# Layer 1's point-cloud loop: VectorE makes the low part of 4 of 16 slots, from a high part that ScalarE copies to PSUM; GpSimd makes the rest

## The chip, the cores and the metric

One core of a Trainium2 chip runs the whole program in one launch. The metric is device time in microseconds (us), the median of the runs. Names in the profile: PE is TensorE's matmuls and PEld its weight loads, DVE is VectorE, ACT is ScalarE, POOL is GpSimd, SP is the engine that issues most DMAs. L1894 is line 1894 of the kernel file.

## What is computed

Two rows of 64 tokens (1024 wide) go through six residual blocks: a quantised cross product, a state-space mixer, a mixture of LoRA experts, a point-cloud attention, a block-sparse product and a gated feed-forward block. The change lies in the fourth, the point cloud. Its 1024 points (per batch entry, with 64 features each) are sorted by four space-filling keys, and every point looks at a window of 10 neighbours in each order:

```python
neigh = gather(feats, inds)
gf = jnp.concatenate([jnp.broadcast_to(center, (B, N, k, C)), neigh - center], axis=-1)
...
qh = x16.reshape(B * N, k, nheads, headdim)
scores = jnp.einsum('bihd,bjhd->bhij', qh, qh) / np.float32(np.sqrt(headdim))
attn = jax.nn.softmax(scores, axis=-1)
out = jnp.einsum('bhij,bjhd->bihd', attn, qh).reshape(B * N, k, total)
fused = out @ W_lin.T + b_lin
...
h1 = _lrelu(_instance_norm(h1, (2, 3)))
feats1 = h1.max(axis=-1)
```

This is done twice (layer 1 and layer 2), the second time on the features that the first gave; then one more convolution joins both.

## The kernel before

**Where the loop stands.** Each layer first sorts (one-hot products on TensorE) and then runs a loop of 43 steps, 24 points a step. The five engines each run their own program; semaphores alone order them. `walk` writes out the first 8 and the last 3 steps (and 6 more to drain) and turns the 32 between into a hardware loop of four steps a turn, so each engine takes a branch once in four steps. `lagged(n)` means that an engine works n steps behind the loop's number.

**What one step does, by engine** (all tiles have 128 partitions; a step's weights are 16 slots of 30 columns, 480 in all):

- GpSimd, step *it*: `normalise(it)` multiplies the exponentials S by the reciprocal row sums (L2043); `differences(it + 3)` makes the 960 neighbour-minus-centre values X of three steps ahead (L2025); `low_part(it)` subtracts the rounded weights from S and rounds the rest (L2050).
- ScalarE, step *it*: `high_part(it - 1)` rounds S to 16 bits (L1782), `exponentials(it)` (L1789), `unload(it - 4)` copies the weighted rows out of PSUM (L1774), and then a transposing DMA of X is issued (L1796).
- VectorE, step *it*: `reduce(it - 6)` takes statistics and a maximum of the finished rows (L1874, L1880); `shift(it)` takes the maximum of the scores and subtracts it (L1892, L1894); `turn(it - 2)` transposes the weights in 32 x 32 blocks (L1907); `denominators(it)` sums the exponentials and takes the reciprocal (L1914, L1916).
- TensorE, step *it*: `scores(it)` (L1586, L1594), `weighted_rows(it - 4)` (L1614), `linear(it - 5)` (L1635, L1643).
- SP, step *it*: four DMAs place the transposed weights P_turned into PT, a block-diagonal tile (L1523).

**High and low part.** The 32-bit weights are used as two 16-bit halves, interleaved in PP: index 0 of the last axis is the rounded value, index 1 what the rounding left. The products of both are added on TensorE. The two lines in question:

```python
sc.copy(c.PP[ph % 2][:, :, 0:ROWS, 0], c.S[ph % 2][:, :, :]).then_inc(s_hi, 1)
...
gp.tensor_tensor(PP[:, :, 0:ROWS, 1], c.S[ph % 2][:, :, :], PP[:, :, 0:ROWS, 0], ALU.subtract).then_inc(s_lo, 1)
```

**Who waits for whom.** S, PP, P_turned and PT exist twice, so `shift(it)` waits for the low part of step it - 2 (semaphore c_P_low), `turn(it)` for the low part of its own step, `normalise(it)` for the reciprocal (c_den), `low_part(it)` for the high part (c_P_high), `weighted_rows(it)` for the DMAs into PT and for the unload of the step before. The scores have one set of PSUM banks (0, 1), the weighted rows banks 3 and 4, the finished rows 5 and 6. Banks 2 and 7 are used while sorting and not in the loop's even part.

Of the kernel before, what the change touches and what calls it, by code (L numbers as in the profile page):

```python
# [9 lines left out]
ALU = mybir.AluOpType  # L10
# [1249 lines left out]
FIRST = 2 * PHASES  # L1260
LAST = 3
EARLY = STEPS - 5
SOON = N // 4
AHEAD = 3
TURN_LAG, PV_LAG, LINEAR_LAG, REDUCE_LAG = 2, 4, 5, 6
# [89 lines left out]
class Cloud:  # L1355


    def __init__(self, k, ctx):
        sb = lambda name, shape, dt=F32: k.sb(name, shape, dt, ctx)
        made = k.cloud  # L1360
        self.iota, self.PP, self.rows_u, self.cols_v = made.iota, made.PP, made.rows_u, made.cols_v
        self.X_more = [k.hT[:, 4 * u:4 * u + 4, :].bitcast(F16) for u in range(PHASES - len(made.X))]
        self.X, self.X_zeros = made.X + self.X_more, k.sem("c_X_zeros")
        self.conv_d, self.blocks, self.f16, self.WC = made.conv_d, made.blocks, made.f16, made.WC
        slots = lambda first, count: k.ring[:, first:first + count, :].rearrange("p a n -> p (a n)")
        self.spl = slots(9, 1).bitcast(F16).rearrange("p (s t c) -> p s t c", s=2, t=NT)
        self.both = sb("f16_both", [P, B, N + STEP], F16)
        self.fsg = slots(7, 2).rearrange("p (t d) -> p t d", t=NT)
        self.fsg_late = slots(10, 1).rearrange("p (t d) -> p t d", t=NT // 2)
        self.W = N + WIN - 1 - LEAD  # L1370
        self.fsT = sb("sortedT", [P, 4, self.W])
        self.pre = sb("first_windows", [P, 4, LEAD, WIN])
        self.fTr = k.ring[:, 0:4, :]
        self.S = [sb(f"S{u}", [P, 2 * SLOTS, ROWS]) for u in range(2)]
        self.mx = [sb(f"mx{u}", [P, 2 * SLOTS]) for u in range(2)]
        self.den = [sb(f"den{u}", [P, 2 * SLOTS]) for u in range(2)]
        self.PT = k.PT
        self.PC = [sb(f"P_turned{u}", [P, 2 * SLOTS, 32, 2], F16) for u in range(2)]
        self.XR = [x.rearrange("p (s d) -> p s d", s=SLOTS) for x in (slots(7 + u // 2, 1).bitcast(F16)[:, u % 2 * N:(u % 2 + 1) * N] for u in range(PHASES))]
        self.OT = [sb(f"OT{u}", [P, 2, B, COLS]) for u in range(2)]  # L1380
        self.step_sems = [k.sem(f"c_{i}") for i in ("X", "scores", "max", "shifted", "exp", "den", "P", "P_high", "P_low", "P_turned",
                                                    "PV", "O", "H", "reduced")]
        self.placed = [k.sem(f"c_P_placed{u}") for u in range(2)]
        self.rows_in = [k.sem(f"c_X_rows{u}") for u in range(PHASES)]
        self.order_sems = [k.sem(f"c_{i}") for i in ("split", "f16", "second_parts", "centre_copied", "perm",
                                                     "ordered", "rows", "sorted_turned", "sorted_copied", "windows")]
        self.layer_sems = [k.sem(f"c_{i}") for i in ("std", "early_statistics", "first_centres")]
        self.weight_sems = k.sem("c_weights"), k.sem("c_weights_rest")
        self.rows_kept, self.kept = k.rows_kept, k.sem("c_rows_kept")
        self.stats = sb("stats", [P, B, STEPS, 6])  # L1390
        self.partial = sb('early_mean_variance', [P, B, 2])
        self.mvb, self.stdb, self.rsb, self.shift, self.cb = sb("mvb", [P, B, 2]), sb("stdb", [P, B]), sb("rsb", [P, B]), sb("shift", [P, B]), sb("cb", [P, 1])
        self.bias, self.o_bias = sb("end_bias", [P, B]), sb("o_bias", [P, 1])
        self.end_sems = [k.sem(f"c_end_{i}") for i in ("bias", "scaled")]
        self.f1, self.f2 = k.ring[:, 4, :], k.ring[:, 5:7, :]
        self.lin_n, self.lin_c, self.conv, self.blin = made.lin_n, made.lin_c, made.conv, made.blin

        self.o_stats, self.o_mv, self.o_std, self.o_rs = sb("o_stats", [P, 2, 6]), sb("o_mv", [P, 2]), sb("o_std", [P, 1]), sb("o_rs", [P, 1])
        self.conv_2, self.flag = sb("conv3_last", [P, C]), sb("block_flags", [P, KC * 32])
        self.conv3_in = k.sem("conv3_in")  # L1400
        self.WN = sb("WN", [P, 2, B, P])

        self.wparts, self.wrest = sb("WC_parts", [P, 3, P], BF16), sb("WC_rest", [P, P])


def stage_cloud_layer(nc, k, dr, c, layer):
    O = C * layer
    nb = 1 if layer == 1 else B
    with ExitStack() as ctx:
# [31 lines left out]
        t0 = STEPS * (layer - 1)  # L1441
        s_PT, s_XR = c.placed, c.rows_in

        def placed(it, ph):

            before = (layer - 1) * (STEPS - STEPS // 2 if ph % 2 == 0 else STEPS // 2)
# [12 lines left out]
        if layer == 2:  # L1459
            s_both = sem("f16_both")  # L1460
            s_early = sem("early_products")
            s_conv, s_ost, s_ostd, s_ox = (sem(i) for i in ("last_convolution", "out_statistics", "out_std", "out_x"))
            res = c.fsg[:, 0:NT // 2, :].rearrange("p t d -> p (t d)")
        n = Norm(k, 3) if layer == 1 else None
        turns = n.turns if n else lambda count: count
# [215 lines left out]
        def _(act):  # L1681
# [94 lines left out]
            def high_part(it, ph):  # L1776
# [4 lines left out]
                    act.wait_ge(s_turned, t0 + it - 1)  # L1781
                sc.copy(c.PP[ph % 2][:, :, 0:ROWS, 0], c.S[ph % 2][:, :, :]).then_inc(s_hi, 1)  # L1782

            def exponentials(it, ph):
                if not inside(it):
                    return
# [11 lines left out]
            def step(it, lagged):  # L1798
                high_part(*lagged(1))
                exponentials(*lagged(0))  # L1800
                unload(*lagged(PV_LAG))
                turn_rows(*lagged(0))
                if isinstance(it, int) and it < NM - 1:
# [14 lines left out]
                    sc.activation(raw_piece(i), raw_piece(i), ACT.Identity, bias=c.bias[:, b:b + 1], scale=c.rsb[:, b:b + 1]).then_inc(s_scaled, 1)  # L1818
            if layer == 2:
                act.wait_ge(s_ost, 3)  # L1820
                sc.activation(c.o_std[:, :], c.o_mv[:, :][:, 1:2], ACT.Sqrt, bias=k.eps[:, 0:1]).then_inc(s_ostd, 1)
                act.wait_ge(s_bias, bias0 + 2)
                sc.activation(res[:, HALF:], ps[:, 1, :], ACT.Identity, bias=c.o_bias[:, 0:1], scale=c.o_rs[:, 0:1]).then_inc(s_scaled, 1)

# [2 lines left out]
        def _(v):  # L1827
# [68 lines left out]

            words = lambda x: x[:, :, :, :].rearrange("p s j w -> p (s j w)").bitcast(F32)

            def turn(it, ph):
                if not inside(it):  # L1900
                    return
                v.wait_ge(s_lo, t0 + it + 1)
                if draining(it):
                    v.wait_ge(s_PT[ph % 2], placed(it - 2, ph))
                elif after(it, 2):
# [12 lines left out]
            def step(it, lagged):  # L1918
                reduce(*lagged(REDUCE_LAG))
                shift(*lagged(0))  # L1920
                turn(*lagged(TURN_LAG))
                denominators(*lagged(0))
                if isinstance(it, int) and it > STEPS:
                    early_statistics(it)

# [39 lines left out]
            if layer == 2:  # L1965
# [2 lines left out]
                    vec.bn_stats(c.o_stats[:, half, :], ps[:, half, :]).then_inc(s_ost, 1)  # L1968
                v.wait_ge(s_ost, 2)
                vec.bn_aggr(c.o_mv[:, :], c.o_stats[:, :, :]).then_inc(s_ost, 1)  # L1970
                v.wait_ge(s_ostd, 1)
                vec.reciprocal(c.o_rs[:, :], c.o_std[:, :]).then_inc(s_ost, 1)
                v.wait_ge(s_ost, 4)
                vec.scalar_tensor_tensor(out=c.o_bias[:, :], in0=c.o_mv[:, 0:1], scalar=-1.0, in1=c.o_rs[:, :], op0=ALU.mult, op1=ALU.mult).then_inc(s_bias, 1)
# [15 lines left out]
        def _(pool):  # L1990
            gp = nc.gpsimd
            if layer == 1:
                for more in c.X_more:
                    gp.memset(more, 0.0).then_inc(c.X_zeros, 1)
                pool.wait_ge(k.PT_zeros, 32)
                pool.wait_ge(c.X_zeros, len(c.X_more))
            pool.wait_ge(s_soon, soon0 + 16 * B * NHEAD)

            def first_differences():
# [45 lines left out]
            def low_part(it, ph):  # L2045
# [1 line left out]
                    return  # L2047
                PP = c.PP[ph % 2]
                pool.wait_ge(s_hi, t0 + it + 1)
                gp.tensor_tensor(PP[:, :, 0:ROWS, 1], c.S[ph % 2][:, :, :], PP[:, :, 0:ROWS, 0], ALU.subtract).then_inc(s_lo, 1)  # L2050

            def step(it, lagged):
                normalise(*lagged(0))
# [116 lines left out]
```

## Time and profile before

| | us |
|---|---|
| median of 3 runs (994.27 to 994.8) | 994.58 |
| the profiled execution | 993.34 |
| its span in the profile | 991.7 |
| busy over the span: TensorE | 922.2 (93%) |
| VectorE | 733.9 (74%) |
| GpSimd | 452.0 (46%) |
| ScalarE | 392.1 (40%) |
| L2050, low part, 86 instructions (both layers) | 97.9, mean 1139 ns |
| L2043, normalise, 86 instructions | 86.7, mean 1008 ns |
| L1782, high part, 86 instructions | 66.9, mean 778 ns |

A busy share over the whole span mixes stages with different limits, so the table says little about one loop. Layer 1's loop lies between about 498 and 680 us of the span, layer 2's between about 714 and 905. The times of the profile are those of one execution; 993.34 - 991.7 = 1.64 us of it lie outside the profiled span.

### The profile page before, as it was taken

To read this page: it belongs to the slowest core of one execution; us is meant where nothing else is said; L and a number is where in the kernel's file an instruction comes from. 1 tells how busy PE (TensorE), PEld (TensorE's weight loads), DVE (VectorE), ACT (ScalarE), POOL (GpSimd) and SP (SyncE) were. 2 spreads that over 40 slices of the span, in tenths; PEclk is the share of its full clock that TensorE was granted. 3 is DMA by queue.
4 is the path that set the end of the run, shared out by engine and by line. 5 is a ranking of instruction groups with operands and counts; after the bars stand their busy time and mean duration, and the time that the engine had idled before them with its cause. 6 is when DMAs were issued, how large, how long until landed. Compare 5 with 4: busy or idle time off the path is not lost. (4 is left out here: it accounts for less than half of the span.)

```text
span 991.7 us, 36771 instructions
## 1 busy us (share of the span) xinstructions
PE 922.2 (93%) x15278; PEld 701.0 (71%) x15279; DVE 733.9 (74%) x1931; ACT 392.1 (40%) x679; POOL 452.0 (46%) x410
## 2 busy tenths in 40 slices
PE   4899899999999999999978988879989999999998
PEld 2799879696969687765965666657955656665695
DVE  7698738866657483897967989886879999997410
ACT  6343414141433323212354555554355555553010
POOL 1101212531211202020299999980499999986000
PEclk9999999999999999999998999999979999999999
DMA  9998797888878796566257666672357665662650
GB/s 365 407 408 308 259 337 261 294 304 295 312 273 308 258 353 224 188 260 255 93 89 128 130 141 134 134 138 63 109 104 126 127 127 125 126 128 46 262 247 22
DMA packets 148961, 204.95 MB, mean 207 GB/s; under 512 B 99409, under 2 KB 101137, under 8 KB 148498
## 3 DMA queue, kind: packets, MB, share of 16 engines
q1 hardware_dynamic: 55058, 172.06, 48.9%
q10 hardware_dynamic: 91392, 23.34, 14.2%
q0 software_dynamic: 2432, 8.42, 2.4%
q8 instruction: 59, 0.97, 0.4%
q14 instruction: 20, 0.16, 0.0%
HBM read 154.45 MB, written 1.61 MB: 157 GB/s over the span
## 5 line engine op out<-in xcount | busy, mean ns | idle before, releaser
L546 PEld LDWEIGHTS ps<-hT,ring 128*128 128x128 f32 x2304 | 258.1, 192 | 6.7 <-issue 5.7
L546 PE MATMUL ps<-hT,ring 128*128 128x128 f32 x2304 | 260.0, 275 | 0.8 <-ACT xc L692 0.8
L1614 PE MATMUL ps<-PT,ring 128*64 128x120 f16 x2752 | 100.0, 225 | 27.8 <-ACT OT L1774 14.1
L1782 ACT CAST PP<-S 128x480 f16<-128x480 f32 x86 | 66.9, 778 | 125.4 <-POOL S L2043 125.4
L1614 PEld LDWEIGHTS ps<-PT,ring 128*64 128x64 f16 x2752 | 87.0, 113 | 37.8 <-issue 27.4
L978 POOL TENSOR_TENSOR y_y<-y_z,sgate 128x512 f32<-128x512 f32 x16 | 20.1, 1272 | 193.0 <-DVE y_z L909 193.0
L579 PE MATMUL ps<-wt,y_n 128*128 128x512 f32 x224 | 99.4, 596 | 1.4 <-DVE xs L901 1.4
L2050 POOL TENSOR_TENSOR PP<-S,PP 128x480 f16<-128x480 f32 x86 | 97.9, 1139 | 5.7 <-ACT PP L1782 5.7
L2043 POOL TENSOR_TENSOR S<-S,den 128x480 f32<-128x480 f32 x86 | 86.7, 1008 | 16.9 <-DVE den L1916 15.8
L808 DVE SCALAR_TENSOR_TENSOR xc<-xpad,parg,xc 128x128 f32<-128x128 f32 x192 | 59.3, 372 | 42.2 <-ACT xc L692 41.0
L1774 ACT COPY OT<-ps 128x960 f32<-128x960 f32 x86 | 81.2, 944 | 12.5 <-PE ps L1614 12.5
L2025 POOL TENSOR_TENSOR X<-sortedT,ring 128x960 f16 (+1 forms) x42 | 79.4, 1891 | 0.5 <-DMA ring<-X 0.5
L1639 PE MATMUL ps<-OT,WN 128*128 128x480 f32 x172 | 77.9, 576 | 0.0
L2025 POOL TENSOR_TENSOR hT<-sortedT,ring 128x960 f16 (+2 forms) x42 | 77.4, 1842 | 0.0
L579 PEld LDWEIGHTS ps<-wt,y_n 128*128 128x128 f32 x224 | 41.4, 190 | 48.7 <-issue 48.6
L1892 DVE TENSOR_REDUCE mx<-ps 128x16 f32<-128x480 f32 x86 | 56.1, 652 | 17.5 <-PE ps L1594 8.8
L1789 ACT ACTIVATE S<-S 128x480 f32<-128x480 f32 x86 | 51.6, 600 | 32.8 <-DVE S L1894 32.6
L1914 DVE TENSOR_REDUCE den<-S 128x16 f32<-128x480 f32 x86 | 56.0, 651 | 11.2 <-ACT S L1789 8.3
L1874 DVE BATCH_NORM_STATS2 stats<-ps 128x240 f32 (+2 forms) x129 | 47.5, 396 | 21.8 <-PE ps L1639 9.5
L1907 DVE STREAM_TRANSPOSE P_turned<-PP 128x512 f32<-128x512 f32 x86 | 60.4, 702 | 3.0 <-PE ps L1614 2.4
L1894 DVE TENSOR_TENSOR S<-ps,mx 128x480 f32<-128x480 f32 x86 | 56.6, 658 | 3.0
L834 DVE TENSOR_SCALAR_CACHE_REDUCE junk<-krow,kcol 128x1024 bf16<-128x1024 f32 (+3 forms) x64 | 51.7, 808 | 0.6 <-DVE kcol L824 0.2
(328 smaller groups left out, 1478.6 us busy)
## 6 DMA issues: line engine op xcount, KB each, us to landing
ring<-in_w_in SPq DMA_DIRECT2D x36, 2048.0 KB, 9.3
wt<-in_w_out SPq DMA_DIRECT2D x14, 2048.0 KB, 7.8
PT<-P_turned SPq DMA_DIRECT2D x332, 64.0 KB
ring<-in_w SPq DMA_DIRECT2D x8, 1024.0 KB, 12.9
ctx_chunks<-in_ctx SPq DMA_DIRECT2D x4, 1024.0 KB, 8.8
krow<-keys_scratch POOLq DMA_DIRECT2D x8, 512.0 KB, 7.5
mchunk<-in_mask_t POOLq DMA_DIRECT2D x8, 512.0 KB, 8.7
ring<-in_w_out SPq DMA_DIRECT2D x2, 2048.0 KB, 8.0
```

The lines of the kernel that those rows point to most:

```text
L546: mm = nc.tensor.matmul(ps[:, bank, j * T:(j + 1) * T], weights[:, j, kc * P:(kc + 1) * P], k.hT[:, kc, :], start=kc == 0, stop=kc == KC - 1)
L579: mm = nc.tensor.matmul(ps[:, 6 + c, :], rows[:, j, :], weights[:, j, c * HALF:(c + 1) * HALF], start=j == 0, stop=j == GB - 1)
L808: vec.scalar_tensor_tensor(out=dst, in0=src, scalar=params(j, tap), in1=dst, op0=ALU.mult, op1=ALU.add).then_inc(s_cv, 1)
L1614: mm = nc.tensor.matmul(ps[half, out_bank(it) + slot // 4, at:at + 4 * ROWS], XR[:, slot, half], PT[:, :, r * SLOTS + slot, 0:ROWS, part], ...
L1639: mm = nc.tensor.matmul(H, c.WN[:, a, 0, :], OT[:, a, :, :], start=False, stop=a == 1)
L1774: sc.copy(c.OT[ph % 2][:, :, :, :].rearrange("p a b n -> p a (b n)"), ps[:, out_bank(it):out_bank(it) + 2, 0:2 * COLS]).then_inc(s_O, 1)
L1782: sc.copy(c.PP[ph % 2][:, :, 0:ROWS, 0], c.S[ph % 2][:, :, :]).then_inc(s_hi, 1)
L1894: vec.tensor_tensor(S[:, :, :].rearrange("p (r s) i -> p r s i", r=2), scores, fcopy(c.mx[u][:, :], [[SLOTS, 2], [1, SLOTS], [0, ROWS]]), ...
L1907: vec.transpose(words(c.PC[ph % 2]), words(c.PP[ph % 2])).then_inc(s_turned, 1)
L2025: ins = gp.tensor_tensor(fcopy(c.X[u][:, 0, 0:1], full(cnt)), fcopy(c.fsT[:, 0, bass.ds(it * STEP, 1)], trio(start, cnt, 1)), fcopy(c.fTr[ ...
L2043: gp.tensor_tensor(S, S, fcopy(c.den[ph % 2][:, :], [[1, 2 * SLOTS], [0, ROWS]]), ALU.mult).then_inc(s_P, 1)
L2050: gp.tensor_tensor(PP[:, :, 0:ROWS, 1], c.S[ph % 2][:, :, :], PP[:, :, 0:ROWS, 0], ALU.subtract).then_inc(s_lo, 1)
```

## The change

In layer 1 alone the 16 slots are divided. GpSimd makes the low part of slots 0 to 11 (360 columns). ScalarE, behind each step's exponential, copies the rounded high part of slots 12 to 15 (120 columns) from PP to PSUM, in bank 2 or 7 by the step's parity. VectorE, at the end of each step, subtracts that copy from S and writes the low part of these slots. The transpose waits for both. Two new semaphores, c_P_high_share and c_P_low_share, carry the order; two old ones are given up for them (X_zeros is counted on `filled`, and out_std on the layers' shared `std`), with the same waits.

```diff
+SHARE, SHARE_BANK = slice(12, 2 * SLOTS), (2, 7)
...
+        shared = layer == 1
+        shares = [k.ps[:, bank, 0:(SHARE.stop - SHARE.start) * ROWS].rearrange("p (s i) -> p s i", i=ROWS) for bank in SHARE_BANK]
...
+            def high_share(it, ph):
+
+                if not inside(it) or not shared:
+                    return
+                if after(it, 2):
+                    act.wait_ge(c.low_share, t0 + it - 1)
+                act.wait_ge(s_hi, t0 + it + 1)
+                sc.copy(shares[ph % 2], c.PP[ph % 2][:, SHARE, 0:ROWS, 0]).then_inc(c.high_share, 1)
...
                 high_part(*lagged(1))
                 exponentials(*lagged(0))
+                high_share(*lagged(1))
                 unload(*lagged(PV_LAG))
...
+            def low_share(it, ph):
+
+                if not inside(it) or not shared:
+                    return
+                v.wait_ge(c.high_share, t0 + it + 1)
+                vec.tensor_tensor(c.PP[ph % 2][:, SHARE, 0:ROWS, 1], c.S[ph % 2][:, SHARE, :], shares[ph % 2], ALU.subtract).then_inc(c.low_share, 1)
...
                 v.wait_ge(s_lo, t0 + it + 1)
+                if shared:
+                    v.wait_ge(c.low_share, t0 + it + 1)
...
                 denominators(*lagged(0))
+                low_share(*lagged(1))
...
-                gp.tensor_tensor(PP[:, :, 0:ROWS, 1], c.S[ph % 2][:, :, :], PP[:, :, 0:ROWS, 0], ALU.subtract).then_inc(s_lo, 1)
+                mine = slice(0, SHARE.start if shared else 2 * SLOTS)
+                gp.tensor_tensor(PP[:, mine, 0:ROWS, 1], c.S[ph % 2][:, mine, :], PP[:, mine, 0:ROWS, 0], ALU.subtract).then_inc(s_lo, 1)
```

VectorE's program in layer 1's hardware loop, one of the four steps of a turn, before (the line numbers are those of each kernel's own file; in brackets the semaphores waited for):

```order
L1874 ISA [waits c_H]
L1874 BN_STATS stats<-ps 128x6
L1880 ISA
L1880 TENSOR_REDUCE ring<-ps 128x24
L1888 REGISTER_ALU
L1892 TENSOR_REDUCE mx<-ps 128x16 [waits c_P_low,c_scores]
L1894 TENSOR_TENSOR S<-ps,mx 128x480 [waits c_max]
L1907 STREAM_TRANSPOSE P_turned<-PP 128x512 [waits c_PV,c_P_low]
L1914 TENSOR_REDUCE den<-S 128x16 [waits c_exp]
L1915 ISA
L1916 RECIPROCAL den<-den 128x16 [waits c_den]
```

The same step of VectorE's program in the changed kernel:

```order
L1889 ISA [waits c_H]
L1889 BN_STATS stats<-ps 128x6
L1895 ISA
L1895 TENSOR_REDUCE ring<-ps 128x24
L1903 REGISTER_ALU
L1907 TENSOR_REDUCE mx<-ps 128x16 [waits c_P_low,c_scores]
L1909 TENSOR_TENSOR S<-ps,mx 128x480 [waits c_max]
L1931 STREAM_TRANSPOSE P_turned<-PP 128x512 [waits c_PV,c_P_low_share,c_P_low]
L1938 TENSOR_REDUCE den<-S 128x16 [waits c_exp]
L1939 ISA
L1940 RECIPROCAL den<-den 128x16 [waits c_den]
L1919 TENSOR_TENSOR PP<-S,ps 128x4x30 [waits c_P_high_share]
```

One instruction of 4 x 30 columns now stands between the reciprocal and the next step's statistics, and the transpose has one semaphore more.

ScalarE's program for the same step, before (CAST at L1782 is the high part, COPY at L1774 the unload):

```order
L1782 CAST PP<-S 128x16x30 [waits c_P_turned,c_P]
L1787 REGISTER_ALU
L1789 ACTIVATE S<-S 128x480 [waits c_shifted]
L1774 COPY OT<-ps 128x960 [waits c_H,c_PV]
L1796 DMA_TRANSPOSE ring<-hT 128x8x128
```

And in the changed kernel:

```order
L1787 CAST PP<-S 128x16x30 [waits c_P_turned,c_P]
L1801 REGISTER_ALU
L1803 ACTIVATE S<-S 128x480 [waits c_shifted]
L1796 CAST ps<-PP 128x120 [waits c_P_high,c_P_low_share]
L1779 COPY OT<-ps 128x960 [waits c_H,c_PV]
L1810 DMA_TRANSPOSE ring<-hT 128x8x128
```

The copy to PSUM stands between the exponential and the unload, so the unload and the transposing DMA are issued behind it.

## Rows read from the trace of the kernel before

**Rows 1.** Stretch, its length; busy PE, PEld, DVE, ACT, POOL; clock; DMA share; GB/s.

```profile
556.00:656.00 100.00, 86.55 (x2834) 61.36 (x2830) 89.67 (x182) 53.97 (x78) 100.00 (x78) 1.00 0.65 136
```

**Rows 2.** GpSimd's timeline over layer 1's loop: start us, length us, what.

```profile
502.49 0.99 POOL L2043 TENSOR_TENSOR S<-S,den 128x480 f32<-128x480 f32 x1 [0.39 <-DVE den L1916]
...
521.84 0.99 POOL L2043 TENSOR_TENSOR S<-S,den 128x480 f32<-128x480 f32 x1
...
538.37 0.98 POOL L2043 TENSOR_TENSOR S<-S,den 128x480 f32<-128x480 f32 x1
...
551.84 1.00 POOL L2043 TENSOR_TENSOR S<-S,den 128x480 f32<-128x480 f32 x1
...
652.37 1.06 POOL L2043 TENSOR_TENSOR S<-S,den 128x480 f32<-128x480 f32 x1
653.32 1.94 POOL L2025 TENSOR_TENSOR X<-sortedT,ring 128x960 f16<-128x960 f32 x1
655.16 1.19 POOL L2050 TENSOR_TENSOR PP<-S,PP 128x480 f16<-128x480 f32 x1
656.22 1.07 POOL L2043 TENSOR_TENSOR S<-S,den 128x480 f32<-128x480 f32 x1
657.18 0.90 POOL L2025 TENSOR_TENSOR hT<-sortedT,ring 128x360 f16<-128x360 f32 x1
657.94 0.45 POOL L2030 MEMSET hT<- 128x344 f16 x1
```

**Rows 3.** Waits from 560 to 640: us in total, times, longest.

```profile
ACT PP L1782 <- POOL S L2043: 37.6, 21, 1.9
...
PE ps L1614 <- ACT OT L1774: 10.6, 20, 0.7
...
DVE mx L1892 <- POOL PP L2050: 1.2, 6, 0.2
```

**Rows 4.** VectorE's timeline, layer 1's loop, across a branch.

```profile
562.56 0.25 DVE L1916 RECIPROCAL den<-den 128x16 f32<-128x16 f32 x1
563.08 0.42 DVE L1874 BATCH_NORM_STATS2 stats<-ps 128x240 f32 x1 [0.26 <-issue]
...
563.72 0.65 DVE L1892 TENSOR_REDUCE mx<-ps 128x16 f32<-128x480 f32 x1
564.40 0.66 DVE L1894 TENSOR_TENSOR S<-ps,mx 128x480 f32<-128x480 f32 x1
...
565.83 0.65 DVE L1914 TENSOR_REDUCE den<-S 128x16 f32<-128x480 f32 x1 [0.15 <-ACT S L1789]
566.51 0.25 DVE L1916 RECIPROCAL den<-den 128x16 f32<-128x16 f32 x1
...
570.38 0.25 DVE L1916 RECIPROCAL den<-den 128x16 f32<-128x16 f32 x1
570.54 0.37 DVE L1874 BATCH_NORM_STATS2 stats<-ps 128x240 f32 x1
```

**Rows 5.** VectorE's timeline, layer 2's loop.

```profile
804.77 0.66 DVE L1894 TENSOR_TENSOR S<-ps,mx 128x480 f32<-128x480 f32 x1
...
806.10 0.65 DVE L1914 TENSOR_REDUCE den<-S 128x16 f32<-128x480 f32 x1
...
821.52 0.66 DVE L1894 TENSOR_TENSOR S<-ps,mx 128x480 f32<-128x480 f32 x1
```

**Rows 6.** VectorE's timeline, a small subtraction ahead of layer 2.

```profile
688.51 0.28 DVE L1839 TENSOR_TENSOR WC_rest<-ps,WC_parts 128x128 f32<-128x128 f32 x1
688.71 0.61 DVE L1293 TENSOR_SCALAR ring<-iota,rank 128x512 f16<-128x512 f16 x2
```

**Rows 7.** ScalarE's timeline, layer 1's loop.

```profile
607.67 0.60 ACT L1789 ACTIVATE S<-S 128x480 f32<-128x480 f32 x1
608.17 0.94 ACT L1774 COPY OT<-ps 128x960 f32<-128x960 f32 x1
```

**Rows 8.** TensorE's timeline, a stall early in layer 1's loop.

```profile
540.30 1.14 PE L1614 MATMUL ps<-PT,ring 128*64 128x120 f16 x32 [2.21 <-DMA PT<-P_turned]
```

More of the change, by code:

```diff
@@ L1362, in __init__ @@
         self.X_more = [k.hT[:, 4 * u:4 * u + 4, :].bitcast(F16) for u in range(PHASES - len(made.X))]
-        self.X, self.X_zeros = made.X + self.X_more, k.sem("c_X_zeros")
+        self.X = made.X + self.X_more
         self.conv_d, self.blocks, self.f16, self.WC = made.conv_d, made.blocks, made.f16, made.WC
@@ L1383, in __init__ @@
         self.placed = [k.sem(f"c_P_placed{u}") for u in range(2)]
+        self.high_share, self.low_share = k.sem("c_P_high_share"), k.sem("c_P_low_share")
         self.rows_in = [k.sem(f"c_X_rows{u}") for u in range(PHASES)]
@@ L1461, in stage_cloud_layer @@
             s_early = sem("early_products")
-            s_conv, s_ost, s_ostd, s_ox = (sem(i) for i in ("last_convolution", "out_statistics", "out_std", "out_x"))
+            s_conv, s_ost, s_ox = (sem(i) for i in ("last_convolution", "out_statistics", "out_x"))
             res = c.fsg[:, 0:NT // 2, :].rearrange("p t d -> p (t d)")
@@ L1820, in _ @@
                 act.wait_ge(s_ost, 3)
-                sc.activation(c.o_std[:, :], c.o_mv[:, :][:, 1:2], ACT.Sqrt, bias=k.eps[:, 0:1]).then_inc(s_ostd, 1)
+                sc.activation(c.o_std[:, :], c.o_mv[:, :][:, 1:2], ACT.Sqrt, bias=k.eps[:, 0:1]).then_inc(s_std, 1)
                 act.wait_ge(s_bias, bias0 + 2)
@@ L1970, in _ @@
                 vec.bn_aggr(c.o_mv[:, :], c.o_stats[:, :, :]).then_inc(s_ost, 1)
-                v.wait_ge(s_ostd, 1)
+                v.wait_ge(s_std, std0 + nb + 1)
                 vec.reciprocal(c.o_rs[:, :], c.o_std[:, :]).then_inc(s_ost, 1)
@@ L1993, in _ @@
                 for more in c.X_more:
-                    gp.memset(more, 0.0).then_inc(c.X_zeros, 1)
+                    gp.memset(more, 0.0).then_inc(k.cloud.filled, 1)
                 pool.wait_ge(k.PT_zeros, 32)
-                pool.wait_ge(c.X_zeros, len(c.X_more))
+                pool.wait_ge(k.cloud.filled, 16 + len(c.X_more))
             pool.wait_ge(s_soon, soon0 + 16 * B * NHEAD)
```

## The prediction

> **What bounds the kernel now.** The busy table by stretch comes first: in the 100 us from 556 to 656, the even part of layer 1's loop, GpSimd is busy 100.00, VectorE 89.67, TensorE 86.55, ScalarE 53.97, at a granted clock of 1.00 [rows 1]. So read GpSimd's timeline. Its three instructions of a step start one behind the other: normalise to differences 0.95 us, differences to low part 1.84, low part to the next normalise 1.06, together 3.85, and from the start at 551.84 to that at 656.22 there are 27 steps, 3.866 each [rows 2]. (Instructions overlap a little, so I count from start to start, not by length.) The waits say the same from the other side. ScalarE waited 37.6 us for GpSimd's normalise in 21 steps, VectorE's score maximum for GpSimd's low part in 6 of them, and TensorE 0.53 us a step for ScalarE's unload of the weighted rows [rows 3]. GpSimd itself waits for nobody there. A shorter low part therefore shortens the step until the next engine has no slack.
>
> That next engine is VectorE. What can its step shrink to? Follow its starts [rows 4]: row sums to reciprocal 0.68 (566.51 - 565.83), reciprocal to statistics 0.16 (570.54 - 570.38), statistics to score maximum 0.64 (563.72 - 563.08), maximum to subtraction 0.68 (564.40 - 563.72). From the subtraction to the row sums ScalarE's exponential lies between; in layer 1 this took 1.43, but there the exponential stood behind a high part that GpSimd had released late. Layer 2 shows it without that: 1.33 (806.10 - 804.77) [rows 5]. The sum is 3.49. Once in four steps, at the loop's branch, reciprocal to statistics takes 0.52 (563.08 - 562.56) in place of 0.16, so 0.09 more on the mean: 3.58. That VectorE can run such a ring without a further pause is seen in layer 2, where it has more to do (two statistics a step): four steps from 804.77 to 821.52 are 4.19 each [rows 5], though TensorE is nearly full there too. So GpSimd's 3.866 stands over a VectorE floor of 3.58, and only 0.29 us a step is free.
>
> **The change part by part.**
>
> GpSimd's low part goes from 480 to 360 elements a partition. The differences give a slope: 960 elements take 1.84 to the next start, the 360 of the last step 0.76, so 1.80 ns an element [rows 2]; 120 elements less save 0.22. Pro rata of 1.06 they save 0.27. I take 0.24: GpSimd's own step becomes 3.63.
>
> VectorE gets one subtraction of 120 elements a step, 43 in all, behind the reciprocal and ahead of the next step's statistics, on the ring just summed. The nearest row is a subtraction with one operand in PSUM, 128 elements: it lasts 0.28, and the next instruction starts 0.20 after it [rows 6]. What counts on a full engine is start to start, so 0.19 for 120. In the one step of four with the branch, the sequencer spends 0.52 there already, and the new instruction can run inside that; I charge 0.10. Mean: (3 x 0.19 + 0.10) / 4 = 0.17, and VectorE's step becomes 3.75. Bounds: 0.14 (0.19 in three steps, nothing in the fourth) and 0.28 (the whole length, always), so 3.72 to 3.86. The wait added to the transpose is for VectorE's own subtraction of a step earlier, done long before; it costs nothing while the subtraction itself isn't late.
>
> A rule of the Trainium skill speaks against the change here. Its page "VectorE: DVE Perf Modes", section on the TRN2 errata, gives a VectorE instruction with a PSUM source 120 + N cycles at 0.96 GHz, a fixed cost that small instructions pay each time. For N = 120 that would be an estimated 0.25 us; by it VectorE's step would be 3.83 and the loop's gain a third of what I take. The row's 0.28 of length agrees with the page, its 0.20 to the next start doesn't carry all of it, and the sum goes by the row.
>
> ScalarE gets one copy of 120 elements a step, between the exponential and the unload. Its exponential of 480 lasts 0.60 and its copy of 960 0.94 [rows 7], so 0.26 fixed and 0.71 ns an element: 0.34 long, some 0.25 in its queue. It starts about 0.50 after the exponential (608.17 - 607.67, where the unload starts now) and is done at 0.9. VectorE wants it at 0.60 (the exponential's length) + 0.68 + 0.16 = 1.44 after the exponential's start at the earliest. So half a microsecond covers it. Behind it stand the unload and the transposing DMA of ScalarE's queue. The unload becomes 0.25 later, and TensorE's weighted rows wait for it. But a late weighted row reaches VectorE only through two more TensorE passes and the scores of two steps on, and TensorE idles 0.53 a step now [rows 3]; I cost it at nothing, at most 0.12 a step (0.25 over two steps) if that cover were gone.
>
> The merged semaphores and the two PSUM banks touch no order in the loop. Layer 2 runs as before.
>
> **Sum.** The loop's step is the larger of 3.63 and 3.75: 0.116 less, times 27 steps = 3.1 us. Ahead of them lie 12 steps. The first five run at GpSimd's pace (502.49 to 521.84, 3.87 each), without statistics on VectorE [rows 2]; but then TensorE waits for transposed weights to land, so only the low parts ahead of the transpose that it waits for count, two times 0.24. Three more, between the stalls, gain 0.12 each. Together 0.8, with 0 and 12 x 0.24 = 2.9 as ends. In the last three steps one shorter low part (-0.24) meets one more subtraction (+0.19): nothing. Total 3.9 us. Everything behind layer 1 is a chain from its last row, so it comes through whole. The profiled execution took 993.34, 1.2 below the median of 994.58, with a span of 991.7; 3.9 off it is 989.4, and off the median **990.7**.
>
> **The rivals.**
>
> *GpSimd stays the bound.* VectorE's new subtraction would have to vanish in its idle tenth (89.67 of 100 busy). Then 0.24 x 27 = 6.5, plus 1.2 ahead: 7.7 less, 986.9. Against it: the ring takes 3.58 without the subtraction, so only 0.05 would be left for it under 3.63, where it needs 0.19 from start to start. 0.08.
>
> *VectorE takes back what GpSimd gives.* The subtraction costs its whole length of 0.28 in every step, the branch's too: 3.86, the old step. Only the start keeps some 0.8 to 1: 993.7, no measurable change. For it: the skill's page above, and that the branch step's 0.52 may not overlap. Against: the reciprocal, 0.25 long, has the next instruction 0.16 behind its start [rows 4]. 0.22.
>
> *Slower: transposed weights come too late.* TensorE's weighted rows need the DMA from the transposed tile. At 540.30 it waited 2.21 us for one [rows 8]; the three steps around it took 13.47 (538.37 to 551.84) in place of 11.60, so one such stall costs 1.9 us. A transfer has about two steps' time, 0.23 less than now. In the even part none was late in 21 steps [rows 3], but the first twelve steps show that they can be. Two more stalls eat the gain, three make 994.58 - 3.9 + 5.6 = 996.3. The DMA queues carry the same bytes in less time, at a busy share of 0.65 [rows 1]. 0.13.
>
> *Slower through the new ScalarE copy* (it lands later than 1.44 after the exponential, and VectorE waits with the statistics behind it) needs 0.5 us more than worked out; 0.03, within the same time.
>
> **How the numbers follow.** My forecast has 0.54, and its own range is 989 to 992.5 (VectorE's price 0.14 to 0.22, and 0 to 2 us of the start). Within 0.2% (2.0 us, about what a measurement here can tell from no change) lie the second rival and the forecast's weak end. Faster 0.64, same 0.21, slower 0.15. The range for 8 in 10 takes in the second rival, half of the first and a stall or two of the third: 987.4 to 995.2.
>
> **What would show it.** GpSimd's low part about 0.85 to 0.9 long, and GpSimd no longer at 100%: its normalise should wait some 0.1 us for VectorE's reciprocal, as nowhere in the even part now. VectorE near 97%, its steps at 3.67 and the branch step near 3.95, mean 3.75; the new subtraction 0.28 long, the statistics 0.19 behind it, no wait for ScalarE's copy. TensorE still idles ahead of the weighted rows. Wrong would be: a step of 3.63 with GpSimd full (first rival), 3.86 with VectorE full (second), or waits of TensorE for the transposed weights between 556 and 656 (third).

## The result and the profile after

| | before | after |
|---|---|---|
| median, us (4 executions each, same chip) | 994.42 (993.67 to 994.8) | 988.89 (987.62 to 990.41) |
| ratio, 95% interval | | 0.9948 [0.9929, 0.9966] |
| profiled execution / its span | 993.34 / 991.7 | 990.41 / 988.8 |

The kernel became 5.5 us faster, 0.56%; forecast were 3.9 us. The view to open first is again the busy table by stretch, here for the even part of layer 1's loop (columns as in [rows 1]):

```profile
550.00:650.00 100.00, 89.19 (x2956) 62.94 (x2945) 95.32 (x215) 65.28 (x108) 98.18 (x81) 1.00 0.66 141
```

Against [rows 1], GpSimd has gone from 100.00 to 98.18 and VectorE from 89.67 to 95.32. Two engines now share the bound, and neither is at 100. ScalarE has 11 points more, TensorE 2.6. The waits from 556 to 636 say who stands still for whom:

```profile
ACT PP L1787 <- POOL S L2068: 22.6, 21, 1.1
...
PE ps L1619 <- ACT OT L1779: 8.7, 21, 0.7
ACT S L1803 <- DVE S L1909: 3.8, 15, 0.4
...
POOL S L2068 <- DVE den L1940: 0.8, 3, 0.3
```

ScalarE's wait for GpSimd's normalise fell from 37.6 us to 22.6 in 21 steps, and its exponential now waits for VectorE's shifted scores. VectorE's maximum, which waited for GpSimd's low part in [rows 3], no longer does. GpSimd waits for VectorE's reciprocal, but in few steps (3, and 2 more with 0.5 us in all that the same view puts down to TensorE's scores): GpSimd's timeline says in which.

```profile
553.81 1.00 POOL L2068 TENSOR_TENSOR S<-S,den 128x480 f32<-128x480 f32 x1 [0.28 <-DVE den L1940]
...
604.82 0.90 POOL L2076 TENSOR_TENSOR PP<-S,PP 128x360 f16<-128x360 f32 x1
605.66 1.01 POOL L2068 TENSOR_TENSOR S<-S,den 128x480 f32<-128x480 f32 x1
...
609.29 1.01 POOL L2068 TENSOR_TENSOR S<-S,den 128x480 f32<-128x480 f32 x1
...
613.24 1.00 POOL L2068 TENSOR_TENSOR S<-S,den 128x480 f32<-128x480 f32 x1 [0.26 <-DVE den L1940]
...
653.83 1.00 POOL L2068 TENSOR_TENSOR S<-S,den 128x480 f32<-128x480 f32 x1
```

The low part of 360 columns is 0.90 long and 0.84 from start to start (605.66 - 604.82; 1.06 in [rows 2]). A full step is 3.63 (609.29 - 605.66), and the next, where the loop branches, 3.95, with GpSimd idle for 0.26. From 553.81 to 653.83 are the same 27 steps as 551.84 to 656.22 in [rows 2]: 100.02 us in place of 104.38, 3.704 a step in place of 3.866.

VectorE's timeline in the same place shows why the fourth step is longer:

```profile
605.49 0.24 DVE L1919 TENSOR_TENSOR PP<-S,ps 128x120 f16<-128x120 f32 x1
605.63 0.40 DVE L1889 BATCH_NORM_STATS2 stats<-ps 128x240 f32 x1
...
606.94 0.66 DVE L1909 TENSOR_TENSOR S<-ps,mx 128x480 f32<-128x480 f32 x1
...
608.27 0.65 DVE L1938 TENSOR_REDUCE den<-S 128x16 f32<-128x480 f32 x1
608.96 0.25 DVE L1940 RECIPROCAL den<-den 128x16 f32<-128x16 f32 x1
609.12 0.24 DVE L1919 TENSOR_TENSOR PP<-S,ps 128x120 f16<-128x120 f32 x1
609.57 0.42 DVE L1889 BATCH_NORM_STATS2 stats<-ps 128x240 f32 x1 [0.21 <-issue]
```

The new subtraction lasts 0.24 but the next instruction starts 0.14 after it (605.63 - 605.49). At the branch, reciprocal to statistics takes 0.61 (609.57 - 608.96), where it took 0.52 in [rows 4]. VectorE's ring (the chain of its own instructions from one subtraction to the next) is 3.63 in three steps (609.12 - 605.49), as long as GpSimd's own step.

Where the 2.9 us between the two spans went, by the starts of GpSimd's normalises: the loop begins 2.65 us **later** (505.14; 502.49 in [rows 2]), its first 12 steps take 0.68 less, the 27 even ones 4.36 less, the last three 0.37 less, and all behind them 0.14 less: 2.65 - 0.68 - 4.36 - 0.37 - 0.14 = -2.90, and 988.8 - 991.7 = -2.9. The late beginning is TensorE's clock in stretches where the change touches nothing:

```profile
36.00:40.00 4.00, 3.65 (x18) 3.24 (x18) 1.96 (x5) 2.07 (x3) 1.82 (x6) 0.58 1.03 408
469.00:476.00 7.00, 6.86 (x128) 6.77 (x129) 4.83 (x16) 3.01 (x9) 0.00 (x0) 0.76 0.28 107
```

The column behind the five engines is the granted clock: 0.58 and 0.76, where before both stretches had 1.00. By TensorE's timeline the program is 1.13 us late ahead of the second stretch; 10 identity products there take 2.31 us together in place of 1.28, and behind them it is 2.11 late.

### The profile page after: what moved, and what is told of

It reads as the page before. It is cut to its first block and busy times, and to the rows that moved or that the text cites. A ratio compares the mean times of both kernels' runs of the same rounds, so it can differ in the third digit from the quotient of the medians.

```text
span 988.8 us, 36916 instructions
## 1 busy us (share of the span) xinstructions
PE 923.1 (93%) x15278; PEld 702.3 (71%) x15279; DVE 737.8 (75%) x1974; ACT 405.3 (41%) x722; POOL 441.9 (45%) x410
## 5 line engine op out<-in xcount | busy, mean ns | idle before, releaser
L1619 PE MATMUL ps<-PT,ring 128*64 128x120 f16 x2752 | 99.3, 224 | 25.7 <-DMA PT<-P_turned 11.2
L1619 PEld LDWEIGHTS ps<-PT,ring 128*64 128x64 f16 x2752 | 86.2, 112 | 35.8 <-issue 25.4
L2076 POOL TENSOR_TENSOR PP<-S,PP 128x360 f16<-128x360 f32 (+1 forms) x86 | 86.9, 1010 | 6.5 <-ACT PP L1787 6.5
```

The source lines that it names most:

```text
L1619: mm = nc.tensor.matmul(ps[half, out_bank(it) + slot // 4, at:at + 4 * ROWS], XR[:, slot, half], PT[:, :, r * SLOTS + slot, 0:ROWS, part], ...
L2076: gp.tensor_tensor(PP[:, mine, 0:ROWS, 1], c.S[ph % 2][:, mine, :], PP[:, mine, 0:ROWS, 0], ALU.subtract).then_inc(s_lo, 1)
```

## Experiments

Where only one execution was timed, I judge by the steps in the trace ("even" is the 27 steps as above), since single times of one kernel scatter by several us.

**The change again, beside its variants** (no edit).

> The changed kernel again, for its spread and as a yardstick. In the profile of the first run the loop of layer 1 began 2.65 us later than before (505.14 against 502.49), in two places where TensorE's granted clock was low ahead of the loop (0.58 from 36 to 40, 0.76 from 469 to 476). If that is chance, it comes and goes between executions of this one kernel: a time near 990 with it and near 987.7 without it, and an even part of 3.71 us a step in both. If the change itself causes it, every execution has it.

Measured: 990.73 (987.17 to 995.55, 9 executions) against 994.91; ratio 0.997 [0.9946, 0.9994]. Even: 99.97, 3.703 a step. The even part repeats to 0.05 us; the total doesn't, and its spread comes from elsewhere. The two stretches of low clock had 0.68 and 1.00 in this trace, so the low clock comes and goes between executions of this one kernel.

**No subtraction on VectorE.** Its instruction and the two waits for it are taken out.

```diff
-                if after(it, 2):
-                    act.wait_ge(c.low_share, t0 + it - 1)
...
-                if shared:
-                    v.wait_ge(c.low_share, t0 + it + 1)
...
-                low_share(*lagged(1))
```

> VectorE's subtraction and the waits for it are left out, so the low part of slots 12 to 15 is missing in layer 1; GpSimd still makes 360 columns and ScalarE still copies. Theory (GpSimd's own step is 3.63, VectorE's ring 3.49 with 3.86 at the branch, mean 3.58, so VectorE's subtraction of 0.14 is what keeps the changed kernel at 3.71): every step of the even part falls to 3.63, GpSimd is full and the stall at the branch is gone; 27 steps x 0.08 = about 2 us less. Rival (the subtraction is hidden, and the 3.94 of every fourth step comes from another wait): three steps of 3.63 and one of 3.94 stay, mean 3.71.

ScalarE's copy stays; the low part of four slots is missing. Even: 98.02, **3.630** in the mean, with no longer fourth step; 990.81 in one execution. GpSimd's timeline:

```profile
603.92 0.92 POOL L2071 TENSOR_TENSOR PP<-S,PP 128x360 f16<-128x360 f32 x1
604.76 1.03 POOL L2063 TENSOR_TENSOR S<-S,den 128x480 f32<-128x480 f32 x1
...
608.38 1.02 POOL L2063 TENSOR_TENSOR S<-S,den 128x480 f32<-128x480 f32 x1
```

No idle time: GpSimd's own step is 3.63, as worked out, and all that VectorE's part costs in the kernel as changed is 100.0 - 98.0 = 2.0 us of the 6.4 that GpSimd freed (104.38 - 98.02).

**Half of the slots to VectorE.**

```diff
-SHARE, SHARE_BANK = slice(12, 2 * SLOTS), (2, 7)
+SHARE, SHARE_BANK = slice(8, 2 * SLOTS), (2, 7)
```

> VectorE makes 8 of 16 slots (240 columns), GpSimd the other 240. Theory: VectorE's ring binds alone now. Its subtraction takes 0.27 from start to start in place of 0.14, so steps of 3.77 and a branch step of about 4.03, mean 3.83, 3.3 us more than the changed kernel in 27 steps, with GpSimd (3.39 of its own) waiting 0.4 a step. Rival (GpSimd's length decides): the step falls by a further 0.24 to 3.47.

Even: 102.75, 3.806 (3.76 to 3.77, and 3.96 at the branch); 992.68 in one execution. VectorE's timeline:

```profile
605.24 0.38 DVE L1919 TENSOR_TENSOR PP<-S,ps 128x240 f16<-128x240 f32 x1
605.51 0.40 DVE L1889 BATCH_NORM_STATS2 stats<-ps 128x240 f32 x1
...
609.00 0.38 DVE L1919 TENSOR_TENSOR PP<-S,ps 128x240 f16<-128x240 f32 x1
```

Here VectorE alone is the bound, so its ring can be read: 3.76, of which the subtraction takes 0.27 from start to start. That leaves 3.49, the figure that the prediction had put together from single gaps. It is start to start that the ring pays, not the 0.38 of length. The theory's branch step of 4.03 was too long: reciprocal to statistics takes 0.61 there, as with 4 slots, so at the branch the longer subtraction costs no more than the shorter.

**An eighth of the slots to VectorE.** The same line with `slice(14, 2 * SLOTS)`.

> The kernel as changed with 2 of 16 slots for VectorE in place of 4. The output stays the reference's. Theory (the step is the longer of two rings: GpSimd's own work and VectorE's): GpSimd's low part is 420 elements and takes about 0.96 to the next start, so its own step is 0.95 + 1.84 + 0.96 = 3.75; VectorE's ring is shorter than that but in the branch step, and the excess there is made up in the next steps; steps 12 to 39 at 3.75 flat, 1.2 us longer than with 4 slots. Rival (VectorE's fixed cost of one more instruction sets the step whatever its size): 3.67 to 3.70, as with 4 slots.

Even: 101.22, 3.749 a step (3.74 to 3.77), the branch's too; 991.93 in one execution. The subtraction of 60 columns is 0.17 long and 0.08 to the next start. The theory held to the hundredth: GpSimd's 3.75 covers the branch. Between 2 slots (3.75), 4 (3.70) and 8 (3.81) the division as changed is the best of those tried.

**ScalarE's copy ahead of the exponential, VectorE's subtraction ahead of the row sums.**

```diff
-                exponentials(*lagged(0))
                 high_share(*lagged(1))
+                exponentials(*lagged(0))
...
-                denominators(*lagged(0))
                 low_share(*lagged(1))
+                denominators(*lagged(0))
```

> The same work in another order: ScalarE's copy ahead of the exponential, VectorE's subtraction between the transpose and the row sums, where VectorE waits for the exponential in any case. Theory: the subtraction then lies under that wait (some 0.12 free), the ring is 3.49 plus at most 0.06 by which the copy delays the exponential, mean near 3.63, and GpSimd's 3.63 binds: 0.07 x 27 = about 2 us less than the changed kernel. Rival: ScalarE can't start the exponential before the high part has ended and the copy has gone through, which costs 0.2 or more in each step: mean 3.75 or more, slower than the changed kernel.

The theory fell: even 102.89, 3.811 a step, 2.9 us more than as changed; 990.84 (10 executions), ratio 0.9967 [0.995, 0.9983], which the times alone can't tell from the change beside it (990.73). ScalarE's timeline, then VectorE's:

```profile
607.39 0.78 ACT L1787 CAST PP<-S 128x480 f16<-128x480 f32 x1 [1.24 <-POOL S L2068]
608.25 0.26 ACT L1796 CAST ps<-PP 128x120 f32<-128x120 f16 x1
...
608.45 0.60 ACT L1803 ACTIVATE S<-S 128x480 f32<-128x480 f32 x1
```

```profile
607.48 0.66 DVE L1909 TENSOR_TENSOR S<-ps,mx 128x480 f32<-128x480 f32 x1
...
608.68 0.27 DVE L1919 TENSOR_TENSOR PP<-S,ps 128x120 f16<-128x120 f32 x1
609.08 0.65 DVE L1938 TENSOR_REDUCE den<-S 128x16 f32<-128x480 f32 x1
```

VectorE's subtraction did slip into the gap in which it waits for the exponential, but the copy must wait for the high part and pushes the exponential back: it starts 0.97 after the shifted scores do (608.45 - 607.48), against 0.69 in the kernel as changed. From shifted scores to row sums it is 1.60 in place of 1.33, and 3.49 + 0.27 = 3.76 is the mean of the three steps without the branch (3.81, 3.74, 3.74). The copy is free only behind the exponential, where the change has it.

**No copy: VectorE reads the high part from SBUF.**

```diff
-                high_share(*lagged(1))
...
-                v.wait_ge(c.high_share, t0 + it + 1)
-                vec.tensor_tensor(c.PP[ph % 2][:, SHARE, 0:ROWS, 1], c.S[ph % 2][:, SHARE, :], shares[ph % 2], ALU.subtract).then_inc(c.low_share, 1)
+                v.wait_ge(s_hi, t0 + it + 1)
+                vec.tensor_tensor(c.PP[ph % 2][:, SHARE, 0:ROWS, 1], c.S[ph % 2][:, SHARE, :], c.PP[ph % 2][:, SHARE, 0:ROWS, 0], ALU.subtract).then_inc(c.low_share, 1)
```

> The kernel as changed without ScalarE's copy of the high part to PSUM: VectorE's subtraction of the 4 slots takes both inputs from SBUF (the high part that ScalarE has written for all slots) and waits for that. The output stays the reference's. Theory (the copy costs nothing, and where VectorE's input lies costs nothing either): steps 12 to 39 of layer 1 stay at 3.70 us a step (3.63 to 3.64 in three, about 3.95 where the loop branches), the subtraction stays 0.24 long and 0.14 to the next start, GpSimd's three groups stay at 0.99, 1.88 and 0.90 long. Rival (by the Trainium skill, SBUF - State Buffer, Who interferes with whom, a VectorE instruction with two SBUF inputs contends with a GpSimd instruction that reads SBUF): the subtraction, which falls into GpSimd's differences, waits for one of them or holds it up. By the smallest form, one of the two operations is longer by the other's 0.2 us a step, which puts the step at about 3.85 and the loop 4 us later; by the largest, VectorE waits for the rest of a 1.88 us difference, and the step passes 4.5.

Even: 101.22, 3.749 a step (a pattern of 3.64, 3.76, 3.67, 3.96); 988.85 in one execution. VectorE's timeline over four steps, then GpSimd's:

```profile
592.23 0.33 DVE L1918 TENSOR_TENSOR PP<-S,PP 128x120 f16<-128x120 f32 x1
...
596.18 0.24 DVE L1918 TENSOR_TENSOR PP<-S,PP 128x120 f16<-128x120 f32 x1
...
599.81 0.37 DVE L1918 TENSOR_TENSOR PP<-S,PP 128x120 f16<-128x120 f32 x1
```

```profile
591.51 0.89 POOL L2075 TENSOR_TENSOR PP<-S,PP 128x360 f16<-128x360 f32 x1
592.39 1.00 POOL L2067 TENSOR_TENSOR S<-S,den 128x480 f32<-128x480 f32 x1
...
596.35 1.00 POOL L2067 TENSOR_TENSOR S<-S,den 128x480 f32<-128x480 f32 x1 [0.27 <-DVE den L1939]
```

With both inputs in SBUF the subtraction lasts 0.28 to 0.38 in the 18 of 24 steps from 556 to 646 in which a GpSimd instruction runs all through it, and 0.24 in the 6 in which GpSimd is just waiting for the reciprocal. With the high part in PSUM it was 0.24 in all 25 steps from 556 to 648, with GpSimd running in most. The sign is the rival's, the size is far below its forms: 0.045 a step, 1.2 us over the even part. The subtraction meets the end of GpSimd's low part and the start of its normalise, not the inside of the long differences; that this is why the price is so small, no run shows. The Trainium skill, "SBUF — State Buffer", section "Who interferes with whom", states that a VectorE instruction with two SBUF inputs contends with a GpSimd instruction that reads SBUF, and one with at most one SBUF input, outside the modes that use both ports, does not; the lengths agree with both halves. So the detour through PSUM is worth 1.2 us here by the steps, and ScalarE pays for it nothing that they see.

**The same split in layer 2 too.**

```diff
-        shared = layer == 1
+        shared = True
```

> The kernel as changed with the same split in layer 2's loop too. The output stays the reference's. Theory (in layer 2 VectorE's ring already sets the step: after the change it runs there without a pause but for the branch, 4.04 to 4.12 us a step and 4.52 where the loop branches, 4.18 in the mean): the subtraction adds what it added in layer 1, 0.14 in three steps and 0.09 in the fourth, so layer 2's steps go to about 4.31 in the mean and layer 2's loop is 3 to 4 us longer; layer 1's steps 12 to 39 stay at 3.70. Rival (GpSimd, 90% busy there, or TensorE, 98%, sets layer 2's step and VectorE's pauses absorb the subtraction): layer 2's steps stay at 4.18 or fall by up to 0.1, and the loop is as long or 2 to 3 us shorter.

Layer 2's 27 even steps took 115.44 us in place of 112.66: 4.276 a step for 4.173, 2.8 us more; layer 1's stayed (100.20); 995.69 in one execution. VectorE's reciprocals in layer 2, first in the kernel as changed, then here:

```profile
805.03 0.25 DVE L1940 RECIPROCAL den<-den 128x16 f32<-128x16 f32 x1
...
809.05 0.25 DVE L1940 RECIPROCAL den<-den 128x16 f32<-128x16 f32 x1
...
813.13 0.25 DVE L1940 RECIPROCAL den<-den 128x16 f32<-128x16 f32 x1
...
817.65 0.25 DVE L1940 RECIPROCAL den<-den 128x16 f32<-128x16 f32 x1
```

```profile
806.69 0.25 DVE L1940 RECIPROCAL den<-den 128x16 f32<-128x16 f32 x1
...
810.88 0.25 DVE L1940 RECIPROCAL den<-den 128x16 f32<-128x16 f32 x1
...
815.07 0.25 DVE L1940 RECIPROCAL den<-den 128x16 f32<-128x16 f32 x1
...
819.59 0.25 DVE L1940 RECIPROCAL den<-den 128x16 f32<-128x16 f32 x1
```

4.02, 4.08 and 4.52 became 4.19, 4.19 and 4.52. The sign of the theory is right; its price in the branch step is not (nothing in place of 0.09). As changed, the steps of 4.02 to 4.12 between the branches make up for the 4.52, with TensorE busy 97.62 of the 100 us from 800 to 900; with the subtraction they are 4.19 to 4.24 and can't, and TensorE's share falls to 94.86. So the same edit that wins where GpSimd binds loses where VectorE's slack between the branches is already in use.

**Eight steps a turn of the hardware loop, on every engine.**

```diff
-            with eng.Fori(first // PHASES, (STEPS - last) // PHASES) as four:
-                for ph in range(PHASES):
-                    body(four * PHASES + ph, lambda lag, ph=ph: (four * PHASES + (ph - lag), (ph - lag) % PHASES))
+            with eng.Fori(0, (STEPS - last - first) // (2 * PHASES)) as eight:
+                for ph in range(2 * PHASES):
+                    body(eight * (2 * PHASES) + (first + ph), lambda lag, ph=ph: (eight * (2 * PHASES) + (first + ph - lag), (ph - lag) % PHASES))
```

> The kernel as changed with eight steps of the cloud loop written out in each turn of the hardware loop in place of four, on every engine and in both layers, so that the loop branches half as often. The output stays the reference's. Theory (once in four steps VectorE's ring loses 0.3 to 0.45 us to the branch, and it is the ring that sets the step): layer 1's steps go to (7 x 3.635 + 3.94)/8 = 3.67 in the mean, 0.9 us less over 27 steps; layer 2's lose 0.45 once in eight steps in place of once in four, 0.056 a step or 1.5 us; about 2.4 us in all, so 986 to 989 and a ratio to the kernel before near 0.993. Rival (the branch's cost is the fetching of the loop's instructions, which grows with the body, or other engines branch at places that bind then): the branch step is longer by as much as is saved, and the ratio stays at 0.995 to 0.997.

The theory's total fell hard: 1010.11 (1000.31 to 1020.2, 6 executions) against 994.03; the ratio, 1.0119 [1.0082, 1.0155], is that of the four shortest. In one turn the steps are what was expected, 3.63 to 3.66 for seven in a row (571 to 596). Then one takes 9.14; in later turns steps in the middle are long too (up to 6.38), and layer 1's even part is 120.94, 20.9 us more than as changed. Layer 2's, with eight steps a turn as well, is 112.91 (112.66 as changed). TensorE's matmuls at the long step, then one of its weight loads:

```profile
594.02 1.03 PE L1648 MATMUL ps<-OT,WN 128*64 128x240 f32 x8
599.24 0.38 PE L1591 MATMUL ps<-mask_cols,mask_rows 64*128 64x240 bf16 x2 [4.18 <-POOL hT L2050]
...
600.39 1.18 PE L1619 MATMUL ps<-PT,ring 128*64 128x120 f16 x19 [0.15 <-issue]
602.62 0.91 PE L1619 MATMUL ps<-PT,ring 128*64 128x120 f16 x13 [1.05 <-issue]
```

```profile
599.23 0.11 PEld L1591 LDWEIGHTS ps<-mask_cols,mask_rows 64*128 64x128 bf16 x2 [4.61 <-issue]
```

The idle time of the matmuls is put down to GpSimd's differences, but the weight loads of the same line show 4.61 us with nothing waited for ("issue"), and the run of 32 equal matmuls (L1619) breaks off after 19 with nothing to wait for either. The profile's list of DMA queues has one more witness, first as changed, then here, then here for the 2 us from 594 to 596 alone:

```profile
q8 instruction: 59, 0.97, 0.4%
```

```profile
q8 instruction: 84, 1.38, 0.6%
```

```profile
q8 instruction: 2, 0.03, 12.8%
```

25 more packets of instructions were fetched, 16 KB each. Two fall between 594 and 596, where TensorE stops, none between 571 and 593, in the seven regular steps, and 21 in all between 554 and 675. In the kernel as changed none falls between 554 and 653; here none falls between 800 and 898, in layer 2. By the rows a step of layer 1 has 109 matmuls (2 + 64 + 32 + 3 + 8) and as many weight loads, so eight steps have 1,744 instructions without waits and registers; in layer 2 it is 104 and 1,664. The Trainium skill, "Runtime: NRT & Kernel Launch", section "Instruction fetch mechanics", states that an engine streams its program through a small store (2,048 instructions on TensorE, refilled in blocks of 256) and that a branch whose target isn't in the current window of two pages has to wait for the fetch. The trace agrees that a wait goes with a fetch; it does not agree with two pages (an estimated 512 instructions by that section) for TensorE, since the 872 of a turn of four steps were run again and again without one. Which engine's fetches the 25 are, the view doesn't say, and why 1,664 instructions are kept and 1,744 are not, no run shows. So the rival's mechanism held in layer 1, and was far dearer than it had said; the pause at VectorE's branch as changed is another thing, since no fetch goes with it.

**Eight steps a turn on VectorE alone**, and **VectorE without a loop** (its 43 steps written out), to leave TensorE's loop as it is (the lines of `walk` that take these arguments are left out):

```diff
...
-            walk(v, step)
+            walk(v, step, turn=2 * PHASES)
```

```diff
...
-            walk(v, step)
+            walk(v, step, STEPS - LAST, LAST)
```

> The kernel as changed with eight steps a turn of the hardware loop on VectorE alone; the other engines keep four, TensorE among them. The output stays the reference's. Theory (the longer loop failed by TensorE's instructions alone, and VectorE's branch is what costs): layer 1's steps 12 to 39 between 3.64 and 3.67 in the mean with one of 3.95 in eight, 1 to 1.5 us less; layer 2 1.5 us less; 986 to 988 and a ratio near 0.992. Rival (VectorE's own longer body is fetched again in each turn too): its branch pause grows to 1 us or more once in eight steps, and nothing is won.

> The kernel as changed with VectorE's steps of the cloud loop written out one after the other, 43 in a layer, so that VectorE has no hardware loop and no branch there; all other engines keep their loops of four steps. The output stays the reference's. Theory (the pause of VectorE's ring once in four steps is its own branch, and that pause is all that keeps layer 1's step above 3.63 and layer 2's above 4.05): layer 1's steps 12 to 39 at 3.63 to 3.64 flat, 1.8 us less; layer 2's step at 4.05 in place of 4.18, 3 us less over its 27 steps; 984 to 987 in all and a ratio near 0.990. Rival (fetching straight code costs VectorE more than a branch of a loop that it holds, as TensorE's longer loop did with stalls of 2 to 4 us): pauses on issue ahead of VectorE's instructions at several places, steps above 3.70 and a ratio above 0.997. Second rival (the pause belongs to another engine's branch): the step once in four stays at 3.95.

With eight steps: even 99.44, 3.683; steps 20 to 22 are 3.63 to 3.64 and step 23, with the branch, 3.91, so the branch's price didn't grow; layer 2's even part stayed (112.75). 989.75 (12 executions) against 994.13, ratio 0.9947 [0.9924, 0.9971]: beside the change's own 0.9949, no difference that the times can tell.

Without a loop: even 98.11, **3.634** a step (3.63 to 3.67), and GpSimd never waits inside it. Its first and last even normalise:

```profile
552.92 0.99 POOL L2069 TENSOR_TENSOR S<-S,den 128x480 f32<-128x480 f32 x1 [1.11 <-DVE den L1941]
...
651.03 1.02 POOL L2069 TENSOR_TENSOR S<-S,den 128x480 f32<-128x480 f32 x1
```

So the longer fourth step is VectorE's own branch, shown by taking that branch alone away. In layer 2 the theory fell: the even part stayed at 112.63 us, now in steps of nearly one length (4.15 to 4.19 but for the first). TensorE is busy 97.57 of the 100 us from 800 to 900 there, as in the kernel as changed (97.62); what VectorE lost at its branch had been made up in the steps between, so there VectorE's ring did not set the step by itself, as this theory and that of both layers had it. 988.07 (982.93 to 990.6, 7 executions) against 994.13, ratio 0.9912 [0.988, 0.9944].

**The last two, to place this version.**

> The kernel as changed once more, beside the two below. Theory: layer 1's steps 12 to 39 at 3.70 us, as in both of its traces so far; a ratio of 0.994 to 0.997, the rest of its spread from stretches of low granted clock. Rival (there is none on its mechanism): a different figure would only say how wide the spread is.

> The kernel with VectorE's 43 steps written out, once more: layer 1's steps 12 to 39 came to 3.634 us flat and layer 2's stayed at 4.17, 1.9 us less than as changed by the trace. Theory (those 1.9 us are all that it wins): layer 1's steps at 3.63 flat again, layer 2's at 4.17, the three steps that end layer 1's loop at 11.4 as in the kernel as changed (13.7 in the first trace, by transposed weights that came late once), and a ratio of 0.991 to 0.995, near 0.993. Rival (the written-out steps also lose something at the loop's end, each time): the last three steps at 13.7 again and a ratio of 0.994 or more.

As changed, beside the two above: 989.49 (12 executions), ratio 0.9949 [0.9927, 0.9971]; even 100.01. Without VectorE's loop, later: 988.0 (10 executions) against 993.77, ratio 0.9928 [0.9901, 0.9956]; even 98.11 again, the last three steps 11.36, so the 13.74 of its first trace (a TensorE wait of 2.9 for transposed weights) does not come each time. It beats the kernel before, and by the traces the changed one by 1.9 us; the intervals of the two overlap, so from the times alone that is not shown.

## Why the prediction came out as it did

The sign, the place and the mechanism were right; one term of the sum was sized too dear.

- **GpSimd's low part**: forecast 0.24 saved and an own step of 3.63; measured 0.22 (1.06 - 0.84) and 3.63, bare in the kernel without VectorE's part (3.630). Right.
- **VectorE's ring without the subtraction**, 3.49: right (3.76 - 0.27 with half of the slots).
- **VectorE's price** is the step that was mis-sized. I took 0.19 from start to start in three steps from [rows 6], and the branch 0.10, 0.17 in the mean; measured are 0.14 and 0.09 (0.61 - 0.52), 0.13. With 0.14 the ring is 3.63, no longer than GpSimd's own step, so three steps of four lose nothing. The step came to 3.704 in place of 3.75, and the even part to 4.36 us in place of 3.1. The three sizes run here are 0.08, 0.14 and 0.27 from start to start for 60, 120 and 240 columns; the row of 128 columns (0.20) lies 0.05 above that line. Where two engines' steps are this close, these 0.05 made most of the 1.2 us by which the even part beat its forecast.
- **The rule weighed in the prediction** (the Trainium skill, "VectorE: DVE Perf Modes", TRN2 errata: 120 + N cycles at 0.96 GHz) gives an estimated 0.19, 0.25 and 0.38 us for the three sizes. The lengths agree (0.17, 0.24, 0.38). The next instruction starts some 0.1 us before that length is over, in all three, and the ring pays only up to there.
- **ScalarE's copy** at nothing: right, by ScalarE's timeline after.

```profile
607.63 0.60 ACT L1803 ACTIVATE S<-S 128x480 f32<-128x480 f32 x1 [0.17 <-DVE S L1909]
...
608.14 0.25 ACT L1796 CAST ps<-PP 128x120 f32<-128x120 f16 x1
```

The copy is done 0.76 after the exponential's start, and VectorE takes it up at 609.12, 1.49 after. The place is what makes it free: ahead of the exponential, with the subtraction moved too, the even part was 2.9 us longer. TensorE still waits for the unload, 0.41 a step in place of 0.53.

- **The first 12 steps**: forecast 0.8, measured 0.68 in this trace, but 48.6 to 50.2 us in three traces of the same kernel (49.35 before). The agreement is luck: TensorE's waits for late transposed weights between 500 and 556 come and go (4.7 us before; 5.2, 7.1 and 6.6 in the three).
- **The last three steps**: forecast nothing, 0.37 less. They were 11.36 to 11.37 in all three traces of the changed kernel and 11.74 in the one of before.
- **The rivals.** GpSimd as the bound (3.63 flat) came true in three steps of four and needed only VectorE's branch gone to be true in all. VectorE taking it all back fell. Transposed weights too late: TensorE has no such wait from 556 to 654 (one of 0.6 us lies just ahead). ScalarE's copy late fell.
- **The total**: even part and last steps give 4.7 us; the medians gave 5.5, 4.2 and 4.6 on three occasions.

## What to carry to other kernels

On an engine that is nearly full, price a small added instruction by the gap to the next start of the very same form, not by its length nor by a cousin's; and price it against the second ring, since a few hundredths decide whether it is free. Put a copy on a third engine where the instruction behind it is not on that ring. A longer loop body can cost far more than the branches that it saves (20.9 us in layer 1's even part): unroll the one engine that pays for the branch, leave the engine with the most instructions a step alone, and look at the instruction packets.

## What was not expected of the hardware

TensorE's granted clock falls in some executions of the same kernel and not in others, in stretches where the program does the same. From 36 to 40 us it was 1.00 before, 0.58 in the profile after, 0.68 and 1.00 in the other two traces of the changed kernel; from 469 to 476 it was 1.00, then 0.76, 1.00 and 1.00. A mean of 0.58 says that most of the stretch ran at the lower of the two levels, 1.2 GHz in place of 2.4. In the profile after, ahead of the second stretch, TensorE had just waited 1.47 us for VectorE and was running transposes; before, it had waited the same 1.47 at the full clock. So the cause stays open. Over the three traces of the changed kernel the loop starts between 502.45 and 505.14 us, a spread of more than half of what the change wins, which is why the steps of the trace and not single times carry the verdicts here.
